# Plain passes of a graph network: padding visits left out, the last chunk signalled by fours, edge scores in the first 48 visits of a turn

## The reference, cut to what matters

```python
msg = x[edge_src] * norm[:, None]                      # layer 0
agg = jax.ops.segment_sum(msg, edge_dst, num_segments=N)
neigh = jax.ops.segment_sum(feat[src], dst, num_segments=N_NODES)   # layer 2
he = (inputs_edge @ W_edge).reshape(-1, H, DE)          # layer 3
w_e = jnp.einsum('ehd,hd->eh', he, attn_edge)           # the edge scores
```

## Time and profile before

| | us |
|---|---|
| median of 3 runs | 9300.25 (9298.95 to 9302.06) |
| the profiled execution, its own time | 9279.53 |
| its span (first to last instruction) | 9277.8 |
| first plain pass, first gather issued to sums copied | 271.36 to 2368.63 |
| second plain pass, the same | 4785.54 to 6877.21 |

### The profile page before, as it was taken

How to read it: one execution, slowest core, us unless ns; L and a number is a source line. 1 busy time by engine, 2 the same in 40 slices (tenths; PEclk the granted TensorE clock), 3 DMA queues, 4 the chain that set the end, 5 groups by cost and what they waited for, 6 DMA issues and landing times. The chain is left out here.

```text
span 9277.8 us, 87408 instructions
## 1 busy us (share of the span) xinstructions
PE 3990.4 (43%) x18719; PEld 3766.0 (41%) x18720; DVE 1374.1 (15%) x2901; ACT 3150.7 (34%) x8574; POOL 6458.9 (70%) x6800
## 2 busy tenths in 40 slices
PE   6456656566714242433433333333341433424334
PEld 6455656565503242433433333333341332424334
DVE  7100000000330110101230000000012211112125
ACT  1344333434314252433114344343420433424320
POOL 1677777777377777777747777777756777777774
PEclk7555555555555555555555555555555555555555
DMA  2222222222221111111111111111113111111111
GB/s 58 92 55 54 52 55 55 55 53 53 64 64 27 27 27 27 27 27 26 27 24 26 26 26 26 26 26 26 26 20 70 31 31 31 31 31 31 31 31 23
DMA packets 312926, 352.81 MB, mean 38 GB/s; under 512 B 155007, under 2 KB 187813, under 8 KB 309323
## 3 DMA queue, kind: packets, MB, share of 16 engines
q0 software_dynamic: 218064, 232.48, 12.8%
q1 hardware_dynamic: 94640, 117.49, 3.9%
HBM read 309.75 MB, written 42.24 MB: 38 GB/s over the span
## 5 line engine op out<-in xcount | busy, mean ns | idle before, releaser
L770 POOL DMA_INDIRECT rows_l<-table,idx_c_l x3328 | 3140.0, 944 | 1309.0 <-issue 1013.6
L951 POOL DMA_INDIRECT rows_a<-table,idx_c_a x3200 | 3053.1, 954 | 1046.8 <-issue 1046.8
L565 PE MATMUL acc_l<-rows_l,hot_l 128*128 128x65 f32 x6656 | 1495.1, 415 | 1960.6 <-DMA rows_l<-table,idx_c_l 1911.3
L565 PEld LDWEIGHTS acc_l<-rows_l,hot_l 128*128 128x128 f32 x6656 | 1467.4, 332 | 1995.6 <-issue 1995.6
L565 PE MATMUL acc_a<-msg_a,hot_a 128*128 128x66 f32 (+1 forms) x6656 | 1485.9, 423 | 435.7 <-DVE msg_a L1048 224.3
L565 PEld LDWEIGHTS acc_a<-msg_a,hot_a 128*128 128x128 f32 x6656 | 1440.3, 331 | 485.6 <-issue 474.3
L699 ACT ACTIVATE dist_l<-iota,neg_c_l 128x128 bf16<-128x128 f32 x3328 | 1052.1, 386 | 31.1 <-PE acc_l L565 25.6
L699 ACT ACTIVATE dist_a<-iota,neg_c_a 128x128 bf16<-128x128 f32 x2816 | 890.1, 386 | 148.6 <-PE acc_a L565 148.6
L905 ACT ACTIVATE score_a<-score_a 128x128 f32<-128x128 f32 (+1 forms) x28 | 13.1, 469 | 2580.4 <-DVE score_a L1017 2580.4
L1085 PE MATMUL work_a<-ident,rows_a 128*128 128x128 f32 (+1 forms) x70 | 22.4, 444 | 2002.9 <-DMA rows_a<-table,idx_c_a 1988.0
L732 ACT COPY idx_c_l<-src_tl 128x16 int32 (+1 forms) x208 | 42.3, 203 | 2416.7 <-PE acc_l L565 2391.0
(11 more groups left out here) (254 smaller groups left out, 2430.6 us busy)
## 6 DMA issues: line engine op xcount, KB each, us to landing
rows_l<-table,idx_c_l POOLq DMA_INDIRECT x3328, 2.4
rows_a<-table,idx_c_a POOLq DMA_INDIRECT x3328, 2.4
feat<-edge_attr SPq DMA_DIRECT2D x25, 1125.0 KB
feat<-edge_attr SPq DMA_DIRECT2D x25, 937.5 KB
table<-stage SPq DMA_DIRECT2D x49, 260.0 KB, 2.0
spread<-zero SPq DMA_DIRECT2D x12, 832.0 KB, 14.1
starts_l<-spread SPq DMA_DIRECT2D x2, 3328.0 KB, 11.6
target<-target_d SPq DMA_DIRECT2D x5, 832.0 KB, 8.7
```

Of the source, the lines that this page charges most:

```text
L565: return nc.tensor.matmul(acc[:, bass.ds(at, row.shape[-1])], hot, row, start=False, stop=True, skip_group_check=True)
L770: pool.indirect_dma_start(rows[:, s, k, 0:D], None, table, bass.IndirectOffsetOnAxis(idx_c[:, s, k:k + 1], 0)).then_inc(gathered[s], 16)
L951: pool.indirect_dma_start(rows[:, u, k, 0:row], None, table, bass.IndirectOffsetOnAxis(idx_c[:, u, k:k + 1], 0)).then_inc(gathered[u], 16)
```

## The change

1. `VU = T + NB - 1 = 1660` is the number of visits that the plain passes now do. V stays 1664 for the attention passes, which pass V to `keep_sums`; its default is now VU.
2. `steps` writes the body a third time, for the last turn alone (turn 25), with `end = CH - (V - VU) = 12`: the last chunk of this turn has 12 visits instead of 16, for POOL, PE and ACT.
3. In this last chunk the gathers of each four visits add to a semaphore of their own (`gathered_last[0]`, `[4]`, `[8]`), and PE waits for 64 ahead of each four visits in place of one wait for all gathers of the chunk.
4. `at` is `u * (BODY - CH) // UNITS`: the units now stand ahead of visits 0, 4, 8, 13, 17, 21, 26, 30, 34, 39 and 43 of every turn. Chunk 0 and chunk 1 of a turn have four units each (three each before), chunk 2 three (as before) and chunk 3 none (two before).

```diff
--- before.py
+++ after.py
@@ -40,6 +40,7 @@
 EP = T * P
 G = -(-(T + NB - 1) // P)
 V = G * P
+VU = T + NB - 1
 VP = V * P
 CH = 16
 SLOTS = 4
@@ -70,7 +71,7 @@
 HALVES = (0, NB // 2), (NB // 2, NB)
 EPS = 1e-5
 LOW = -3.0e38
-assert E == EQ * PIECES * UNITS * UNIT * 2 and V == BODY * ITERS and T == HCH * HSLOTS * HITERS and NB == BPB * NG
+assert E == EQ * PIECES * UNITS * UNIT * 2 and V == BODY * ITERS and VU % QUAD == 0 and V - VU < QUAD * 2 and T == HCH * HSLOTS * HITERS and NB == BPB * NG
 
 
 class Count:
@@ -544,9 +545,10 @@
 
         def steps(engine, body):
 
-            body(0, True)
-            with engine.Fori(1, ITERS) as i:
-                body(i, False)
+            body(0, True, CH)
+            with engine.Fori(1, ITERS - 1) as i:
+                body(i, False, CH)
+            body(ITERS - 1, False, CH - (V - VU))
 
 
 
@@ -564,9 +566,9 @@
 
             return nc.tensor.matmul(acc[:, bass.ds(at, row.shape[-1])], hot, row, start=False, stop=True, skip_group_check=True)
 
-        def keep_sums(dve, acc, summed, kept, width):
-
-            dve.wait_ge(summed, 1 + V // QUAD)
+        def keep_sums(dve, acc, summed, kept, width, visits=VU):
+
+            dve.wait_ge(summed, 1 + visits // QUAD)
             for b in range(NG):
                 nc.vector.tensor_copy(agg[:, b * BPB:(b + 1) * BPB, 0:width],
                                       acc[:, b * BANK:b * BANK + BPB * AW].rearrange("p (b f) -> p b f", f=AW)[:, :, 0:width])\
@@ -582,7 +584,7 @@
 
             HALF_A = -(-UNITS // 2)
             half = (slice(0, HALF_A * UNIT * 2 * D), slice(HALF_A * UNIT * 2 * D, EC * D))
-            at = [u * BODY // UNITS for u in range(UNITS)]
+            at = [u * (BODY - CH) // UNITS for u in range(UNITS)]
             W = UNIT * P
             C = UNIT * 2 * H
             feat = tsb("feat", [P, EC * D])
@@ -716,6 +718,7 @@
                 acc = tps(f"acc_{tag}", [P, NG * BANK])
                 chunk_ready = sem(f"chunk_ready_{tag}")
                 gathered = [sem(f"gathered_{tag}_{s}") for s in range(SLOTS)]
+                gathered_last = {k: sem(f"gathered_last_{tag}_{k}") for k in range(0, CH - (V - VU), QUAD)}
                 dist_ready = sem(f"dist_ready_{tag}")
                 hot_ready = sem(f"hot_ready_{tag}")
                 summed = sem(f"summed_{tag}")
@@ -732,9 +735,9 @@
                             nc.scalar.copy(idx_c[:, s], src_tl[:, bass.ds(c * CH, CH)]).then_inc(chunk_ready, 1)
                             nc.scalar.copy(neg_c[:, s], neg_tl[:, bass.ds(c * CH, CH)]).then_inc(chunk_ready, 1)
 
-                        def hots(i, s, first):
+                        def hots(i, s, first, end=CH):
                             act.wait_ge(chunk_ready, 2 * (i * SLOTS + s + 1))
-                            for k in range(0, CH, QUAD):
+                            for k in range(0, end, QUAD):
                                 n = s * CH + k
                                 if not (first and n < DEPTH):
                                     act.wait_ge(summed, 1 + i * (BODY // QUAD) + (n - DEPTH) // QUAD + 1)
@@ -756,19 +759,20 @@
                         with act.Fori(2, ITERS) as i:
                             body(i, False, False)
                         for s in range(1, SLOTS):
-                            hots(ITERS - 1, s, False)
+                            hots(ITERS - 1, s, False, CH if s < SLOTS - 1 else CH - (V - VU))
 
                     @block.gpsimd
                     def _(pool):
 
-                        def body(i, first):
+                        def body(i, first, end):
                             for s in range(SLOTS):
                                 want = held(pool, 2 * (i * SLOTS + s + 1))
                                 pool.wait_ge(one, 1)
                                 pool.wait_ge(chunk_ready, want)
-                                for k in range(CH):
-                                    pool.indirect_dma_start(rows[:, s, k, 0:D], None, table,
-                                                            bass.IndirectOffsetOnAxis(idx_c[:, s, k:k + 1], 0)).then_inc(gathered[s], 16)
+                                last = s == SLOTS - 1 and end < CH
+                                for k in range(end if last else CH):
+                                    pool.indirect_dma_start(rows[:, s, k, 0:D], None, table, bass.IndirectOffsetOnAxis(idx_c[:, s, k:k + 1], 0))\
+                                        .then_inc(gathered_last[k // QUAD * QUAD] if last else gathered[s], 16)
 
                         steps(pool, body)
 
@@ -788,13 +792,17 @@
                         zero_sums(acc, summed)
                         pe.wait_ge(one, 1)
 
-                        def body(i, first):
+                        def body(i, first, end):
                             for s in range(SLOTS):
+                                last = s == SLOTS - 1 and end < CH
                                 _, at = nc.values_load_multi_w_load_instructions(
                                     offs[0:1, bass.ds((i * SLOTS + s) * CH, CH)], engines=PE_ONLY, min_val=0, max_val=TOP)
-                                pe.wait_ge(gathered[s], 16 * CH * (i + 1))
-                                for k in range(CH):
+                                if not last:
+                                    pe.wait_ge(gathered[s], 16 * CH * (i + 1))
+                                for k in range(end if last else CH):
                                     n = s * CH + k
+                                    if last and k % QUAD == 0:
+                                        pe.wait_ge(gathered_last[k], 16 * QUAD)
                                     if more and not first:
                                         more.tensor(pe, i, n)
                                     if k % QUAD == 0:
@@ -1061,7 +1069,7 @@
                                             ins.then_inc(hot_ready, 1)
 
                         groups(dve, body)
-                        keep_sums(dve, acc, summed, kept, sums)
+                        keep_sums(dve, acc, summed, kept, sums, V)
 
                     @block.tensor
                     def _(pe):
```

## The result

Eight runs of each kernel: before 9300.24 us (9298.78 to 9302.28), after 9274.26 us (9270.61 to 9275.07). The ratio is 0.9971, with a 95% interval from 0.9962 to 0.998: 26.0 us less, and 9275 was predicted.

The account below looks back on a forecast made before the run. Bound: POOL's unbroken train of gathers in the plain passes, plus the pass ends. 13.3 us (first pass) and 11.7 (second) sum to 25.0, taken off the 9300.25 median: 9275, range 9270 to 9286.

Parts of the forecast that it names:

- The train of gathers as the bound: Plain passes: POOL issues gathers without a hold-up, 1.248 us each; only the ends of the passes can change the time.
- First pass, 13.3 us less: End of first plain pass: DVE's first copy of sums starts at 2350.9 instead of 2364.2 us.
- The read: PE's read of 16 offsets into registers ahead of the last chunk, no longer covered by idle time: 2.0 us.
- Units, 3.8 of it: First pass: two units less after the last landing save 3.8 us; denser chunks earlier in the turn cost nothing.
- Second pass, 11.7 us less: End of second plain pass: DVE starts at 6861.7 instead of 6873.35 us.
- What was named as late next: Second pass: PE waits for the landing of visit 1660, 3.1 us after its issue.
- The third copy at nothing: Last turn's new straight-line code, run once: no cost taken, with 0 to 4.8 us kept for the first pass.
- The slow landing as a matter of the train's end: Rival: the last real gather lands after 4.8 us whatever its indices; 23.3 us saved, 9277; chance 0.12.
- The stall of the third copy: Rival: new code stalls PE by 4.8 and POOL by 5.9 us, or part; 9279 to 9286; chance 0.10.
- The ends are on the path: The rival denied this, or had the gain at pass ends waited for at the barrier behind: 9300; chance 0.07.
- The denser units that hold POOL up: Rival: chunks of four units delay POOL's gathers; 2 us a turn would give 9325; chance 0.05.
- The offset of 20.7 us: Timed median 9300.25 lies 20.7 us above the profiled execution; the saving is taken off the median unchanged.

Follow-up runs that it names:

- f1: The whole change run once more, no other edit, against the kernel before: 9256.6 us against 9281.41, ratio 0.9974.
- f2: The kernel before with only the units moved to the first 48 visits of a turn: 9279.38 us, ratio 0.9997.
- f3: The kernel before with the last turn written out and its four padding gathers reading real visits' rows: 9276.53 us, ratio 0.9995.
- e2: The kernel before with only the last turn written out as a third copy of the body: 11926.57 us, ratio 1.0.
- g1: The kernel before with only the third copy of the body, run again in another set: 11921.38 us, ratio 1.0001.
- f: A set of four follow-up kernels on one chip, with the kernel before beside them at 9281.41 us.
- e1: The kernel before with only the units moved, in a set where before took 11923.21 us: 12171.62 us, ratio 1.0203.
- g4: f4 with the last chunk's offsets read before chunk 0 of the last turn, against the kernel before: 12145.99 us against 11922.62, ratio 1.019.
- f4: The change plus last chunk's offsets read before chunk 2 and attention padding gathers left out, against the kernel before: 9250.8 us, ratio 0.9967.

## Why the prediction was right

**The train of gathers as the bound: right.** 1659 waits of "issue", none over 0.3 us, and the pass is as long as its gathers plus its end. The median moved by 26.0 us where 25.0 were predicted.

**First pass, 13.3 us less: measured 13.27** (f1 against before, at one period). Of it 4.99 are the four gathers and 8.23 the end. The read: 1.99 in after and in f1, 2.0 taken. Twelve visits: 5.17 from start to start, 5.0 taken. Last products: 1.43, as taken. Chunk end to DVE: 8.59, 8.4 predicted. The landing was not waited for.

(The Trainium skill, page "Runtime: NRT & Kernel Launch", section "Instruction fetch mechanics", with its 200 ns per register loaded from HBM, would have had an estimated 3.2 us for this read of sixteen; the trace has 1.99 and 1.91, from SBUF.)

**Units, 3.8 of it: measured alone 3.55** (f2), and nothing in the flow. The chunk of four units took 14.35 us (2291.87 to 2306.22, chunk 0 of the last turn in after), 14.4 predicted.

**Second pass, 11.7 us less: measured 11.88.** PE began the last eight records 3.11 us after the last issue where 3.3 were taken (landing 3.0 and 0.1, not 3.1 and 0.2). What was named as late next was late next.

**The third copy at nothing: right**, by f3, by e2 and g1 for the time, and by the ends of after and f1, in which PE's only idle time of "issue" is the read.

**The rivals.** The slow landing as a matter of the train's end is ruled out by f3. The stall of the third copy did not come. The ends are on the path. The denser units that hold POOL up did not come in the comparison nor in f, but they are what e1 and g4 show. The mechanism was described rightly and its margin wrongly: the 44 us left for ACT were read from a trace in which every hand-off follows within 0.3 us, and a condition in which hand-offs take ten uses them up. It had a price of 25 times each microsecond; each turn then cost 9.8, where 2 had been taken. The changed kernel alone was not run in that condition; e1 and g4 both suggest about 2% slower.

**What was luck and what stays open.** The offset of 20.7 us between profile and median was added to the saving as a constant. It was one only because the timed executions of both kernels seem to have had the slower period. In set f the same two kernels have medians of 9281.41 and 9256.6, so the saving of 25 would have held there, but the forecast of 9275 would have been 18 us too high and its range missed. Parts 1 and 3 were separated by working alone: the sets in which they ran by themselves had PE behind at the ends, so their shares (the gathers' 4.99, the landing's, the groups') rest on the timelines of the whole change. And f4 shows how far the reading of one gap carries: the price of one read held five times, 1.91 to 2.03 us, but two in a row were not two times that, and the rows of before had shown it.

## What to carry to other kernels

Where one engine issues without a pause, a change is worth what it takes off that train plus what it takes off its end, and the end can be added up from rows: landing, last group of work, and whatever the idle time had covered (here a register read of 2.0 us that appears only when the wait goes). Before two profiles are subtracted, compare the period of an operation that both do thousands of times. A rearrangement that wins 3.6 us at one end by living on slack in the middle should be measured more than once: it cost 248 us in a condition where that slack was gone.

## What the runs showed of the hardware

- Where nothing holds the gathers up, their period in a plain pass is 1.2483 us (before, f1, f3, f4) or 1.2507 (after, f2), and stays what it is for a whole execution (the two plain passes of a profile agree to 0.0001). What sets it is not known.
- Four gathers in a row of 128 times the same row land in 3.5, 4.0, 4.7 and 4.8 us (before), one with 86 such rows in 3.1 (3.0 in after and f1), the ordinary ones ahead of them in 2.3 to 2.4; with other indices in the same four places they land in 2.4 to 2.6 (f3).
- One read of 16 offsets into PE's registers costs 1.9 to 2.0 us at the end of a plain pass, where nothing covers it. Two in a row stood for 7.4 to 7.7 us in attention (before, f1) and 8.65 in f4; whether the reads alone make that is open.
- In two sets of three the unchanged kernel took 28% longer at nearly the same granted clock (0.504 to 0.506 against 0.506 to 0.508), with waits of DVE and ACT ended up to ten and more microseconds late; one chip showed both conditions, about 13 minutes apart.
